# A four-stage network in one program: scatters with eight in flight, and an expert loop with one signal a step and deeper stages

## What is computed

```python
x = layernorm(x + state_space_block(x))        # B, L, M = 4, 512, 128: 2048 rows of 128
x = layernorm(x + moe(x))                      # the part that the change touches
x = layernorm(x + attention(x))                # 16 heads of 8 over each sequence
x = layernorm(x + three_dense_layers(x))       # 128 -> 512 -> 512 -> 128

def moe(x):                                    # x: (2048, 128), E = 64 experts, I = 88, top 8
    scores = sigmoid(x @ gate_w.T)
    rw = weights_of_the_top_8(scores)          # 4 of 8 groups, then 8 experts; sum 2.5
    y  = [silu(x @ Wg[e].T) * (x @ Wu[e].T) @ Wd[e].T for e in range(E)]
    return sum(rw[:, e] * y[e]) + shared_expert(x)
```

## Time and profile before

| | us |
|---|---|
| median of 3 runs (714.18 to 726.02) | 719.41 |
| the profiled execution | 719.34 |
| its span | 717.2 |
| outside the span | 2.1 |
| mean granted PE clock | 0.90 of full |

### The profile page before, as it was taken

One profiled execution on the slowest core, in us unless ns is written; L12 is line 12 of the kernel. 1 busy time (PEld: TensorE's weight loads), 2 busy tenths in 40 slices (PEclk: granted clock), 3 DMA queues, 4 the chain that ended last, 5 costly groups with the idle time before them and its releaser, 6 DMA issues.

```text
span 717.2 us, 12460 instructions
## 1 busy us (share of the span) xinstructions
PE 559.3 (78%) x3470; PEld 349.0 (49%) x3471; DVE 485.7 (68%) x1125; ACT 378.2 (53%) x844; POOL 394.9 (55%) x420
## 2 busy tenths in 40 slices
PE   4931970006999999999796699959989999989995
PEld 2330650006999989998675123313323333424453
DVE  5499684003565656677565888869987888778986
ACT  4300420002666656655465776737767777877541
POOL 7330567776666553466657777777756200224552
PEclk9975785556999999999899799989999999999998
DMA  5999751115777757767556335313412310000011
GB/s 186 370 398 259 273 174 48 51 54 153 222 214 221 210 155 215 212 185 201 140 142 185 93 89 155 91 28 113 108 40 77 84 35 1 2 0 1 2 30 30
DMA packets 101861, 94.08 MB, mean 131 GB/s; under 512 B 11014, under 2 KB 86886, under 8 KB 101606
## 3 DMA queue, kind: packets, MB, share of 16 engines
q1 hardware_dynamic: 93630, 76.81, 35.4%
q0 software_dynamic: 8192, 16.79, 8.2%
HBM read 45.92 MB, written 47.19 MB: 130 GB/s over the span
## 4 chain that ended last, share of the span: by engine, by line
POOL 38%; PE 18%; issue 18%; DMA 14%; DVE 10%; ACT 2%; POOLq 0%; DVEq 0%; SPq 0%
POOL xd L503 14%; POOL big L518 8%; DMA xd<-xt,idx 7%; POOL arena L518 5%; DMA big<-od,idx 5%; PE ps L1508 4%; PE ps L1498 4%; PE ps L1488 2%; POOL arena L532 2%; DVE arena L1210 2%; POOL arena L530 2%; DVE st L813 2%; POOL rstd L455 1%; POOL big L532 1%; PE ps L1299 1%
## 5 line engine op out<-in xcount | busy, mean ns | idle before, releaser
L503 POOL DMA_INDIRECT xd<-xt,idx x128 | 128.9, 1007 | 85.0 <-issue 59.3
L1093 DVE TENSOR_REDUCE mx<-ps 128x2 f32<-128x1024 f32 x128 | 151.0, 1216 | 32.7 <-PE ps L1488 32.4
L716 ACT ACTIVATE big<-ps 128x512 f32<-128x512 f32 x256 | 141.3, 598 | 52.5 <-PE ps L1498 49.9
L518 POOL DMA_INDIRECT big<-od,idx x80 | 79.0, 988 | 62.4 <-DMA big<-od,idx 23.7
L1394 PE MATMUL ps<-arena,xbT 128*128 x512 | 101.9, 323 | 0.0
L1404 PE MATMUL ps<-idf,big 128*128 128x128 f32 x256 | 50.9, 282 | 62.5 <-DMA big<-xd 62.5
L1015 DVE TENSOR_TENSOR hm<-sg,ps 128x176 f32<-128x176 f32 x128 | 43.0, 336 | 77.0 <-ACT sg L655 63.4
L1498 PE MATMUL ps<-arena 128*128 128x512 bf16 (+1 forms) x256 | 86.4, 391 | 5.5 <-ACT big L716 4.4
L1019 DVE COPY xbT<-ps 128x256 f32<-128x256 f32 x128 | 53.3, 417 | 53.1 <-PE ps L1404 53.1
L655 ACT ACTIVATE sg<-ps 128x176 f32<-128x176 f32 x128 | 40.6, 317 | 90.9 <-PE ps L1394 86.8
L1488 PE MATMUL ps<-arena 125*128 125x512 bf16 (+1 forms) x256 | 71.9, 395 | 19.3 <-DVE mx L1093 15.9
(11 more groups left out here) (216 smaller groups left out, 873.8 us busy)
## 6 DMA issues: line engine op xcount, KB each, us to landing
xd<-zeros SPq DMA_DIRECT2D x2, 8192.0 KB, 44.5
big<-xd SPq DMA_DIRECT2D x64, 256.0 KB
od<-big SPq DMA_DIRECT2D x64, 256.0 KB
arena<-scr SPq DMA_DIRECT2D x96, 96.0 KB
arena<-w_gu SPq DMA_DIRECT2D x1, 5632.0 KB
scr<-places SPq DMA_DIRECT2D x8, 384.0 KB, 3.0
arena<-w_d SPq DMA_DIRECT2D x1, 2816.0 KB
xd<-xt,idx POOLq DMA_INDIRECT x128, 2.2
```

The lines of the kernel that those rows point to most:

```text
L503: pool.indirect_dma_start(out=xd[f], out_offset=bass.IndirectOffsetOnAxis(ap=idx[:, t, k:k + 1], axis=0), in_=xt[:, t], in_offset=None).th ...
L518: pool.indirect_dma_start(out=slot[:, k], out_offset=None, in_=od[f], in_offset=bass.IndirectOffsetOnAxis(ap=idx[:, t, k:k + 1], axis=0)). ...
L716: act.activation(ering[:, HG * (mt % 2) + h], ps[:, 4 + h % 2, :], ACT.Exp, scale=SCALE).then_inc(exp_ready, 1)
L1093: v.tensor_reduce(mx[:, k, TB * h + 2 * a:TB * h + 2 * a + 2], ps[:, 2 * a:2 * a + 2, :], AX_X, ALU.max).then_inc(s1_free, 1)
```

## The change

Five edits. (1) File 0's ring of scatters has 8 semaphores instead of 4 (`AHEAD_ROWS`); file 1 keeps 4, but is no longer drained after tile 14 and tile 15 (`LAST_DRAINED`). (2) PE gives one signal a step, `step_done`, after its last instruction; ACT, DVE and SP wait for that in place of the four. The order in a step becomes D, T, X, GU, and PE waits no longer for `acc_done`. (3) TH, DN = 5, 8 (were 4, 6); `hm` and `hmT` have 4 slots (were 2); the PSUM banks rotate, three a step ("a" holds D and T, "x", "g"), and the work beside the last steps has bank 7 for itself. DVE copies X before it multiplies. (4) SP issues all four stores of a body one body later, each behind a load. (5) Expert numbers are loaded by fours, at the body's start (2), at u = 1 (2), 3 (2) and 5 (1): 7 loads of 4, for 1 of 12 and 3 of 4.

```diff
-    AHEAD = 12
-    GU, TH, DN = 2, 4, 6
+    AHEAD = 16
+    GU, TH, DN = 2, 5, 8
+    RING = 4
     FLYING = 4
+    AHEAD_ROWS = (TOP_K, FLYING)
+    LAST_DRAINED = NT - 2
+        BESIDE = 7
+        def bank_of(s, u, role):
+            if not isinstance(s, int) or s < EARLY:
+                return (3 * u + "axg".index(role)) % 8
+            if s < NPAIR:
+                return (3 * (s - EARLY) + "axg".index(role)) % BESIDE
+            if s < NPAIR + GU:
+                return {(0, "a"): 6, (0, "g"): 0, (1, "a"): 1, (1, "g"): 2}[s - NPAIR, role]
+            return 4 + (s - NPAIR - GU) % 3
# SP
             def quad_in(r, body, src, at):
-                sp.wait_ge(xt_ready, body * 8 + (2 * r + 2))
+                sp.wait_ge(step_done, body * 8 + (2 * r + 2))
                 for r in range(4):                               # in quads()
                     quad_in(r, body, src, at + r)
-                    if r >= 2:
-                        quad_out(r - 2, body, dst, store + (r - 2))
-                    else:
-                        quad_out(r + 2, body - 1, dst, store + (r - 2))
+                    quad_out(r, body - 1, dst, store + r)
-            for r in range(2):
-                quad_out(r + 2, sum(BODIES) - 2, oq[1], QUADS[1] - 6 + r)
+            for r in range(4):
+                quad_out(r, sum(BODIES) - 2, oq[1], QUADS[1] - 8 + r)
             for o in range(2):
                 write_parts(sp, 0, o)
# POOL
-                        if n >= FLYING and (f == 0 or k >= FLYING):
-                            pool.wait_ge(s_sc[f][n % FLYING], 16 * (n // FLYING))
+                        flying = AHEAD_ROWS[f]
+                        if n >= flying:
+                            pool.wait_ge(s_sc[f][n % flying], 16 * (n // flying))
-                    if f == 1:
+                    if f == 1 and t < LAST_DRAINED:
                         for r in range(FLYING):
                             pool.wait_ge(s_sc[f][r], 16 * (TOP_K // FLYING) * (t - FIRST[f] + 1))
# ACT, one step
+                act.wait_ge(step_done, s + 1)
-                    act.wait_ge(d_ready, s + (NT - DN + 1))
-                    act.wait_ge(th_ready, s + (NT - TH + 1))
-                    act.wait_ge(gu_ready, s + (NT - GU + 1))
+                    if not static or s >= GU + 2:
+                        act.wait_ge(hm_ready, s + (NT - GU - 1))
# DVE, one step: the copy of X (waits step_done) now stands before the product (waits sg_ready)
# PE, one step
+                if static and s >= EARLY:
+                    pe.wait_ge(hm_ready, NT + min(s - TH + 1, NPAIR))
                 if not static or DN <= s:
                     pe.wait_ge(th_copied, s + (NT - DN + 1))
-                    pe.wait_ge(acc_done, s - (DN - 1))
...
-                    ins.then_inc(d_ready, 1)
...
+                if not static or TH + 2 <= s < NPAIR + GU:
+                    pe.wait_ge(th_copied, s + (NT - TH - 1))
...
-                    ins.then_inc(xt_ready, 1)
+                if not static or GU <= s < NPAIR + GU:
+                    pe.wait_ge(x_copied, s - (GU - 1))
...
+                ins.then_inc(step_done, 1)
-                load_ids(-3, 3)
+                NEEDED = {1: (-3, 0), 3: (-2, 1), 5: (2,)}
+                load_ids(-4)
+                load_ids(-1)
-                if s == NPAIR + GU:
+                if s == NPAIR + TH - 1:
                     pe.wait_ge(stack_ready, 1)
-                if NPAIR + GU <= s < NPAIR + TH:
-                    for c in range(2):
-                        max_scores(0, 0, 2 * (s - NPAIR - GU) + c)
+                if NPAIR + TH - 1 <= s < NPAIR + TH - 1 + TB:
+                    max_scores(0, 0, s - NPAIR - TH + 1)
```

More of the change, by code:

```diff
@@ L693, in beside @@
                 if what == "x":
[L694 removed]
+                    turn_in(b, ps[:, BESIDE, :])
                 elif what:
[L696 removed]
+                    qk_in(b, "qk".index(what), ps[:, BESIDE, :])
             for s in range(EARLY, NPAIR + DN):
@@ L1388, in pe_pair @@
                     for a in range(2):
[L1389 to L1396 removed]
+                        ins = pe.transpose(pair_of(s, u, "a", 2 * M, P)[0:KI, a], hm[:, (u - TH) % RING, a], idf[:])
                 if load is not None:
                     load()
+                if not static or TH + 2 <= s < NPAIR + GU:
+                    pe.wait_ge(th_copied, s + (NT - TH - 1))
                 if not static or s < NPAIR:
```

119 lines of the change are left out of this document (48 added, 71 removed).

## The result

| | before | after |
|---|---|---|
| median of 4 executions each, us | 717.6 (714.18 to 726.02) | 726.9 (724.77 to 727.94) |
| ratio, 95% interval | | 1.012 (1.007 to 1.017) |
| profiled execution | 719.34 | 724.77 |
| its span | 717.2 | 722.6 |

The forecast was 715, and the sign is the other one. Between the medians lie 9.3 us, between the two profiled executions 5.4 (the profiled one after is the fastest of its four). What follows accounts for the 5.4; what makes up the rest of the 9.3 these two traces can't show. Four points of the rope (the chain of work that the prediction followed from the scatters to the last normalisation) say where they came from. The last of them, "last rstd on POOL", is where POOL takes up the statistics of the last sequence; what lies behind it, up to the end of the span, is attention and the dense layers.

The account below looks back on a forecast made before the run. The prediction took a chain mostly on POOL, its scatters, gathers and sums, to bound the kernel. 719.3 - 8.25 (scatter waits) - 2.3 (one drain) + 4.6 (deeper stages) + 1.5 (loop tail) = 715, range 710.5 to 722.5.

Parts of the forecast that it names:

- the tail: End of the expert loop: q and k written 4.5 later, less 3.0 slack, delays file 1's first gather by 1.5 (0 to 3).
- What costs nothing: Seven loads of expert numbers, bank rotation, rings of four, DVE's swapped order, larger memsets: hidden, no cost on the rope.
- expert numbers stalling PE: Rival, expert loop: 1.0 a body isn't hidden, file 0's 8 bodies cost 8 less 1.2, giving 721.7; chance 0.05.
- Eight scatters in flight: File 0's scatters on POOL: four early waits for landings go, gaining 8.25, lower bound 0.
- the rival's result: POOL's queue carries no more with eight in flight; only the drain is won, 723.2, slower than before; chance 0.08.
- The joint and the deeper stages: Step 64 to first gather: a wait of some 1.2 and the 1.84 clock loss stay; three steps longer, costing 4.6.
- the first rival: PE keeps full clock at step 64 or doesn't wait: 1.84 won too, 713.0, or 711.5 without tail cost; chance 0.17.

Follow-up runs that it names:

- before_dve_late_b: The kernel before with four extra maxima on VectorE just before those of attention's group 1, 4.7 us in all; 730.8 us, ratio 1.018.
- normalise_early: The changed kernel with the four normalisations of sequence 1 moved ahead of attention's group 0; 723.0 us, ratio 1.004 against the kernel before.
- scatters_alone_b: The kernel before with only the two scatter edits (eight in flight for file 0, two drains dropped in file 1), old loop; 712.7 us, ratio 0.989.
- numbers_at_once: The changed kernel with expert numbers loaded as before (one load of 16 at the start, then three of four); 723.3 us, before 716.6, single executions.

## Why the prediction was wrong

**The step that failed** is the last sentence on the tail: "Attention starts 4.5 late against the gathers, 3.0 against file 1's; DVE waits 7.0 for tile 11, which hides it." Attention's first row is 125.65 behind the first gather where it was 121.17: 4.5 late, as written, and 4.7 late against file 1's gathers. This was held against 7.0 of slack as if a delay kept its size. It did not: DVE's elementwise work moved under POOL's product and sums and stretched from 1.10 to 4.83, the lag of the groups grew from 3.2 to 11 and 13, the slack was used up and POOL waited 4.1 more at sequence 2. What should have been held against the delay is the 2.1 between the end of the normalisations and POOL's product, and the 3.0 by which the statistics of sequence 1 were early. With the 1.9 at sequence 1 and 1.2 of longer POOL work this makes the +7.1. before_dve_late_b (the delay alone does it) and normalise_early (without the collision 5 of the 7 are gone) show it from both sides. The wait for sequence 1's statistics was not in the prediction at all: POOL used to arrive there with DVE's statistics done 3.0 us ahead (404.1, rstd at 407.14), and a relative delay of 4.7 uses that up.

**What costs nothing** is the second: "PE's steps in the loop change from 1.48" was named as a sign of error, and it came. A body takes 12.65, not 12.02. In file 0 the wait at step 64 did cover it, as written (that wait is 1.67). What was not seen is its companion: file 1's drains grew from 10.7 to 14.9, and POOL's spacing of tiles, 12.04 before, went to some 12.7 with PE's bodies. These drains had been taken as a constant of the kernel. On one chip the old loop gives 12.3 and 12.9 and the new one 14.3 and 15.0, so some 2 of the 4.2 go with the loop, and the rest varies from run to run. Whether the longer body stretches the drains, or the load and store that SP now issues back to back, stays open. The rival that came near, expert numbers stalling PE, named the place; its price of 1.0 a body was 0.6, and its cause, the number of loads, is worth under 0.1. What makes the 0.6, the one signal or the depth, is open.

**Eight scatters in flight**: right. No wait in the first 64, 7.6 of the 8.25 won, and scatters_alone_b has the last scatter at 253.15 against 262.75 for the old scatters on its chip, 9.6 of the 10.6 for both scatter edits. The Trainium skill's rule on turns between queue rows (DMA: Bandwidth & Descriptors, Queues, rings and completion order) did not make itself felt here: no scatter had to wait for the one eight before it, and the longest landing was 7.6. But the rival's result, that eight in flight don't pay, holds on the six occasions with the 810 us, by another mechanism than the one named.

**The joint and the deeper stages**: the number was right by luck, 4.6 for 4.6: three errors in it cancel. The granted clock stayed at 1.00 (2.4 GHz) behind step 64, where 0.56 had been, so the 1.84 that the clock had cost was not lost again, as in the first rival:

```profile
262.00:264.00 2.00, 2.00 (x17) 2.00 (x17) 0.67 (x3) 0.86 (x3) 0.00 (x0) 1.00 1.15 345
266.00:268.00 2.00, 2.00 (x19) 2.00 (x18) 1.53 (x4) 1.37 (x6) 0.00 (x0) 1.00 0.48 136
```

But a body's start, with its gap, now lay there:

```profile
261.81 0.43 PE L1401 MATMUL ps<-idf,big 128*128 128x128 f32 x2 [0.47 <-ACT hmT L656]
```

From X of step 64 (259.61) to that of step 66 (263.35) it took 3.74, where two steps without a gap take 2.97 and before took 4.81; 0.8 of the 1.84 went back. So the store was issued 12.59 behind X instead of 9.05, +3.5; and it took 3.45 to land where 2.34 was taken from before, the other 1.1:

```profile
271.79 0.39 ACT big L652
...
272.20 3.45 DMA od<-big
```

**The tail's +1.5** did not come in this trace: file 1's first gather waited 1.47 for the store where 0.95 stand there in any case, so the store cost 0.5, and the gathers and sums of file 0 before it took 0.7 less. Its bounds were 0 and 3. In numbers_at_once and normalise_early that gather waited 2.71 and 3.07 for the store, 1.8 and 2.1 above the 0.95, so the term varies between executions within its bounds.

The sum against the profiled execution: 714.9, +4.7 (scatters and drains), -1.7 (tail), +7.1 (POOL waiting for DVE), -0.2, is 724.8.

## What to carry to other kernels

A wait that an engine shows is slack for a delay only if the delayed work keeps its duration; where VectorE and GpSimd both work out of SBUF, lay their two timelines over each other and shift one by the delay before calling it hidden. Here 2.1 us was the margin, not 7.0. And a wait between two engines sets their phase anew: from there a larger delay gives the same collision, not a worse one. A drain that has stood at 2.1 us in a trace is not a constant: it took 2.1 to 3.7 in the traces here. And of a change with two parts, the better half is worth a run: the scatters alone are 1.1% faster, with the loop the kernel was 1.2% slower on its chip. Where it matters on which chip it runs, both halves have to be seen on more than one: the half that wins here loses 2.8% on the others.

## What was not expected of the hardware

- A VectorE tensor_scalar over 128x128 f32, SBUF to SBUF, four of them: 1.10 and 1.27 us beside GpSimd's indirect DMAs, 4.82 to 4.86 when GpSimd's elementwise work begins right behind their start. Each then ends 0.08 or 0.09 behind one instruction of GpSimd, and takes 0.61 to 2.19.
- On six of eight occasions the kernel before took 809 to 816 us instead of 717 to 722, with the same operation durations. There other engines started their next operation 3 to 15 us late while GpSimd issued indirect transfers back to back (15.40 ahead of a VectorE add of 0.29); between the last scatter and the first gather a body of the old loop took 12.0 again.
- The granted clock did not fall behind PE's wait at step 64 in the four traces of the changed loop on the faster chips (waits of 1.67, 1.72, 1.68 and 1.39), and fell in the three of the old loop (to 0.56 behind 1.79, to 0.50 behind 1.99 and behind 4.30). Whether the wait or what PE did before it makes the difference is open.
